# One stored order of q for scores and relative term, and stage one's norms and bound remainder at other places in the queues

## The reference

```python
q = split_heads(x @ Wq + bq)
k = split_heads(x @ Wk + bk)
v = split_heads(x @ Wv + bv)
scores = jnp.einsum('bhid,bhjd->bhij', q, k)
rel = jnp.einsum('bhid,pd->bhip', q, rel_key)
i = jnp.arange(s)[:, None]
j = jnp.arange(s)[None, :]
rel_idx = jnp.clip(j - i + p - 1, 0, p - 1)
bias = jnp.take_along_axis(rel, jnp.broadcast_to(rel_idx[None, None], (b, h, s, s)), axis=3)
causal = j <= i
logits = jnp.where(causal[None, None], (scores + bias) * scale, -jnp.inf)
attn = jax.nn.softmax(logits, axis=-1)
out = jnp.einsum('bhij,bhjd->bhid', attn, v)
```

## Time and profile before

| what | value |
|---|---|
| median of 3 runs | 739.33 us (736.46 to 739.54) |
| the profiled execution, its own time | 737.71 us |
| its span, first to last instruction | 735.6 us |
| stage one (to the first exponential of stage two) | 107.45 us |
| stage two (to the first matmul of stage three) | 107.45 to 526.89 us |
| mean granted TensorE clock | 0.947 of full speed |

### The profile page before, as it was taken

The page is one execution under the profiler, slowest core; times in us unless marked ns, Lnnn a source line. Parts: engine busy times, 40 slices in busy tenths (PEclk is TensorE's granted clock), DMA queues, the critical chain, the costliest instruction groups (busy, mean ns, idle before and its releaser), DMA issues.

```text
span 735.6 us, 18944 instructions
## 1 busy us (share of the span) xinstructions
PE 645.0 (88%) x8066; PEld 467.9 (64%) x8066; DVE 538.9 (73%) x923; ACT 572.5 (78%) x660; POOL 246.6 (34%) x175
## 2 busy tenths in 40 slices
PE   4877669999999999999999999978799898998993
PEld 2333336676766766867667667655588687786682
DVE  5885787787687877786877777765677568588546
ACT  2794977988989889889898898786577868677573
POOL 2100270360640912705408128010271441731801
PEclk9988767999999999999999999997999999999997
DMA  7487423152241231521412314040300000000001
GB/s 229 113 228 219 134 84 90 38 129 66 51 111 40 71 96 35 130 69 43 106 52 68 100 34 123 27 158 1 101 1 1 0 1 1 1 29 0 6 24 59
DMA packets 39175, 52.82 MB, mean 72 GB/s; under 512 B 5656, under 2 KB 29640, under 8 KB 36680
## 3 DMA queue, kind: packets, MB, share of 16 engines
q1 hardware_dynamic: 39088, 51.58, 25.6%
HBM read 39.00 MB, written 11.81 MB: 69 GB/s over the span
## 4 chain that ended last, share of the span: by engine, by line
PE 53%; DVE 13%; ACT 12%; issue 5%; POOL 2%; DVEq 0%; ACTq 0%; POOLq 0%
PE p_o L1114 16%; PE p_s L1089 13%; PE p_z L1788 8%; PE p_z L1791 8%; DVE probs L1215 6%; ACT probs L1332 6%; PE p_s L1023 5%; POOL hid_lo L1709 1%; DVE res L1969 1%; ACT hid_hi L1892 1%; ACT o_acc L1341 1%; ACT even_b L1036 1%; ACT odd_b L1036 1%; PE p_o L1126 1%; DVE hid_lo L1993 1%
## 5 line engine op out<-in xcount | busy, mean ns | idle before, releaser
L1089 PE MATMUL p_s<-q_sb,k_sb 96*128 96x128 bf16 (+1 forms) x1600 | 172.2, 250 | 9.2 <-ACT probs L1332 3.5
L1332 ACT ACTIVATE probs<-p_s 128x1024 f32<-128x1024 f32 x160 | 156.6, 1017 | 18.5 <-DVE p_s L1224 10.8
L1114 PE MATMUL p_o<-probs,v_sb 128*32 128x128 f32 (+1 forms) x3200 | 159.7, 331 | 7.5 <-ACT o_acc L1341 4.7
L992 POOL TENSOR_SCALAR_AFFINE_SELECT even_b<-even_b 128x2048 f32<-128x2048 f32 x31 | 75.9, 2449 | 259.6 <-ACT even_b L1036 259.6
L1332 ACT ACTIVATE probs<-probs 128x1024 f32<-128x1024 f32 x128 | 133.5, 1055 | 36.1 <-DVE probs L1215 35.8
L1089 PEld LDWEIGHTS p_s<-q_sb,k_sb 96*128 96x128 bf16 x1600 | 113.9, 100 | 68.5 <-issue 30.3
L1215 DVE TENSOR_TENSOR probs<-p_s,even_b 128x1024 f32<-128x1024 f32 x96 | 114.9, 1218 | 16.8 <-PE p_s L1089 16.8
L1114 PEld LDWEIGHTS p_o<-probs,v_sb 128*32 128x32 f32 x3200 | 84.6, 111 | 40.9 <-issue 13.9
L1788 PE MATMUL p_z<-hid_hi,h_hi 128*128 128x512 f32 x256 | 102.1, 399 | 1.7 <-POOL hid_lo L1709 1.7
L1023 PE MATMUL p_s<-q_rows,rel_w 72*128 72x64 bf16 x2048 | 83.8, 196 | 19.6 <-DVE probs L1215 8.7
L1791 PE MATMUL p_z<-hid_lo,h_hi 128*128 128x512 f32 x256 | 100.9, 394 | 0.0
(11 more groups left out here) (182 smaller groups left out, 846.2 us busy)
## 6 DMA issues: line engine op xcount, KB each, us to landing
k_sb<-k_dram SPq DMA_DIRECT2D x48, 192.0 KB
q_sb<-q_dram SPq DMA_DIRECT2D x16, 576.0 KB
q_rows<-qr_dram SPq DMA_DIRECT2D x42, 192.0 KB
q_dram<-q_parts SPq DMA_DIRECT2D x12, 256.0 KB, 3.0
k_dram<-k_parts SPq DMA_DIRECT2D x12, 256.0 KB, 3.2
qr_dram<-q_turned SPq DMA_DIRECT2D x12, 256.0 KB, 3.4
x_all<-in_L_attn_x_dram SPq DMA_DIRECT2D x4, 512.0 KB, 4.4
every<-in_L_ffn_h_w_dram SPq DMA_DIRECT2D x2, 1024.0 KB, 8.3
```

The source lines that it names most:

```text
L992: nc.gpsimd.affine_select(out=far, in_=near, compare_op=ALU.is_ge, fill=0.0, base=-1 - r, pattern=[[0, QB], [-1, MCH * RCH]], channel_mult ...
L1089: last = nc.tensor.matmul(slot[:, c:c + n * BLK], k_sb[hg][:, h * S + j * BLK:h * S + (j + 1) * BLK], ap(q_sb[hg], at, [[HG * S, KROWS], [ ...
L1114: last = nc.tensor.matmul(p_o[32 * h:32 * h + 32, at:at + blocks * BLK], v_sb[hg][:, j, h * 32:(h + 1) * 32], probs[n % PBUFS][:, h, col * ...
L1332: nc.scalar.activation(to, got, ACT.Exp, scale=SCALE).then_inc(t_exp, 1)
```

## The change

One layout of q serves both uses. Place i*128 + r*4 + l of a head (block i, group r of four places, l within the group) now lies at r*32 + i*4 + l: groups of four places of one block, eight blocks side by side. The q parts and the bound's parts are written in this order, `q_rows` is loaded from `q_dram`, and `q_turned`, `qr_dram` and their twelve copies and twelve stores are gone. The two matmuls that read q get other steps on their moving side. The sign of the bound's parts changes (the padding row is -1 now). In stage one `layernorm` of batch b+2 stands at the end of batch b, ahead of `gap` and `shift_rest` of batch b; `low_bits` comes after the middle parts, and `root` between the two halves of ACT's part of the bound. The branch for large scores gets a copy of q back into the natural order.

```diff
+LO = 4
...
-            sp.dma_start(to, ap(qr_dram, u * (UH * S) + half * width,
+            sp.dma_start(to, ap(q_dram, u * (UH * S) + half * width,
...
-    def turned_view(to, part):
-
-        return to[:, part, :].rearrange("p (r i) -> p r i", i=NB)
-
-    def untouched_view(got, part):
-
-        return got[:, part, :].rearrange("p (i r) -> p r i", i=NB)
+    def natural(tile):
+
+        return tile.rearrange("p (i r l) -> p r i l", i=NB, l=LO)
+
+    def mixed(tile):
+
+        return tile.rearrange("p (r i l) -> p r i l", i=NB, l=LO)
+
+    def mixed_half(tile, j):
+
+        return tile.rearrange("p (r i l) -> p i r l", i=NB, l=LO)[:, j * (NB // 2):(j + 1) * (NB // 2)]
 
...
-                for done in (s_qst, s_kst, s_rst):
+                for done in (s_qst, s_kst):
                     sp.wait_ge(done, 16 * PARTS)
-                sp.dma_start(q_rows[:, :], ap(qr_dram, 0, [[DROW, PARTS * HD], [0, PARTS], [1, UH * S]])).then_inc(t_qr[0], 16)
+                sp.dma_start(q_rows[:, :], ap(q_dram, 0, [[DROW, PARTS * HD], [0, PARTS], [1, UH * S]])).then_inc(t_qr[0], 16)
...
-                if not last:
-                    turned(b, part)
...
-        for part in range(PARTS):
-            turned(B - 1, part)
...
-            nc.vector.scalar_tensor_tensor(out=m_parts[:, 1, :], in0=p_tr[0:H, :], scalar=-1.0, in1=m_parts[:, 0, :],
-                                           op0=ALU.mult, op1=ALU.subtract).then_inc(s_mr, 1)
+            nc.vector.tensor_tensor(mixed(m_parts[:, 1, :]), natural(p_tr[0:H, :]), mixed(m_parts[:, 0, :]),
+                                    ALU.subtract).then_inc(s_mr, 1)
...
-            if not last_batch:
-                layernorm(b + 1, False, None if first else lambda: gap(b - 1))
-            else:
+            if not first:
                 gap(b - 1)
-            if not first:
                 shift_rest(b - 1)
...
-            nc.vector.tensor_tensor(q_rest[:, :], qf[:, :], q_parts[:, 0, :], ALU.subtract).then_inc(s_rest, 1)
+            nc.vector.tensor_tensor(mixed(q_rest[:, :]), natural(qf[:, :]), mixed(q_parts[:, 0, :]), ALU.subtract).then_inc(s_rest, 1)
...
+            if b + 2 < B:
+                layernorm(b + 2, False)
...
+        layernorm(1, False)
...
-        def turn_query(b, part):
-            act.wait_ge((s_hi, s_mid, s_low)[part], b * 2 + 1)
-            if b > 0 and part == 0:
-                act.wait_ge(s_rst, 16 * PARTS * b)
-            nc.scalar.activation(turned_view(q_turned, part), untouched_view(q_parts, part),
-                                 ACT.Identity).then_inc(s_turned, 1)
-
         def batch(b, first, last_batch):
...
-            if not first and not last_batch:
-                root(b + 1)
...
-            if b < CHECKS:
-                low_bits(b)
...
-            nc.scalar.activation(q_parts[:, 0, :], qf[:, :], ACT.Identity).then_inc(s_hi, 1)
+            nc.scalar.activation(mixed(q_parts[:, 0, :]), natural(qf[:, :]), ACT.Identity).then_inc(s_hi, 1)
             act.wait_ge(s_kf, b + 1)
             nc.scalar.activation(k_parts[:, 0, :], kf[:, :], ACT.Identity).then_inc(s_hi, 1)
-            if not last_batch:
-                turn_query(b, 0)
...
-            if not last_batch:
-                turn_query(b, 1)
-
+
+            if b < CHECKS:
+                low_bits(b)
             if not first:
                 act.wait_ge(s_mst, b * 16)
             for j in range(2):
+                if j == 1 and b + 2 < B:
+                    root(b + 2)
                 act.wait_ge(s_u, b * 2 + j + 1)
-                nc.scalar.activation(m_parts[:, 0, j * 512:(j + 1) * 512], p_tr[0:H, j * 512:(j + 1) * 512],
-                                     ACT.Identity, scale=-1.0).then_inc(s_mneg, 1)
-            if not last_batch:
-                turn_query(b, 2)
+                nc.scalar.activation(mixed_half(m_parts[:, 0, :], j),
+                                     p_tr[0:H, j * 512:(j + 1) * 512].rearrange("p (i r l) -> p i r l", i=NB // 2, l=LO),
+                                     ACT.Identity).then_inc(s_mneg, 1)
             if last_batch:
                 for c in range(FIRST_BEFORE, FIRST_ACT):
                     copy_act(act, "even", c)
                 nc.scalar.activation(exp_warm[:, :], ident[:, 0:1], ACT.Exp, scale=0.0)
-                turn_query(b, 0)
-                turn_query(b, 1)
-                turn_query(b, 2)
 
         root(0)
         transposed(0, True)
...
-        q = q_rows[:, :].rearrange("k (h r i) -> k r h i", h=UH, i=NB)
+        q = q_rows[:, :].rearrange("k (h r i l) -> k r l h i", h=UH, i=NB, l=LO)
...
-            last = nc.tensor.matmul(slot[:, x * QB:(x + 1) * QB], rel_w[0:ROWS, w0:w0 + BLK], q[:, r, :, :],
+            last = nc.tensor.matmul(slot[:, x * QB:(x + 1) * QB], rel_w[0:ROWS, w0:w0 + BLK], q[:, r // LO, r % LO],
                                     start=True, stop=True)
         last.then_inc(t_rel, 1)
 
@@ -1085,10 +1058,10 @@
...
-                    at = h * S + i * BLK
+                    at = h * S + i * LO
...
-                                            ap(q_sb[hg], at, [[HG * S, KROWS], [2 * BLK, n], [1, BLK]]),
+                                            ap(q_sb[hg], at, [[HG * S, KROWS], [2 * LO, n], [NB * LO, BLK // LO], [1, LO]]),
...
-            if u == 0 and hg == 0:
-                act.wait_ge(s_rst, 16 * PARTS * B)
...
```

40 lines of the change are left out of this document (18 added, 22 removed).

## The result

The changed kernel is slower: median 779.16 us (778.72 to 781.02, 4 runs) against 738.08 us (736.46 to 739.54, 4 runs) for the kernel before on the same chip, a ratio of 1.056 (95% interval 1.0537 to 1.0581). The forecast of 730 had the sign wrong, and the time lies far outside its range. The profiled execution took 779.4 us, with a span of 777.5.

A forecast was written before the change was run, and what follows sets the result against it. TensorE was taken to set the pace in stage two, a chain of handovers in stage one. The profiled 737.7 us less 9.5 (6.8 + 2.7) is 728.2; plus 1.6 for the median, 729.8, said as 730; range 725 to 739.5, the forecast's own 727 to 733.

The forecast's parts named there:

- TensorE's moving reads: Stage two's 1920 relative matmuls and the scores: reads in new steps cost nothing; bounds nothing to 110 us in all.
- The slow rival: Stage two: TensorE pays for steps of 8 bytes, 29 ns a matmul, 56 us, kernel 786 us; chance 0.12.
- the 9.5 us of stage one: Stage one's whole gain: 6.8 from an earlier start of batch 3's bound plus 2.7 from its shorter matmuls.
- GpSimd's masks: End of stage one: six masks start at 79.8, end at 98.1, 2.0 us before DVE's first biased addition is due.
- The bound of batch 3: End of stage one, on PE: starts near 82.2, takes 5.4 us instead of 8.1 at the upper clock, 2.7 gained.
- its first rival: Stage one: clock stays low in batch 3, or stores land later; 732.5 to 735 us, chance 0.13.
- The stores: Batch 1, stage one: eight stores become six, the awaited one lands near 68.0 instead of 72.0, 4.0 us gained.
- `kf` of batch 3: Stage one, on ACT: ends at 77.1, 7.4 us earlier, 3.4 of it from the three copies.
- the handover of batches 0 and 1: Stage one, DVE: `root` no longer behind a turned copy; 1.0 us less in batch 0, 1.7 in batch 1.
- Writes in the new order: Stage one, `q_parts` part 0 and `q_rest`: 16-byte f32 read runs cost nothing; up to 3.6 us at 0.9 each.
- the last three copies: End of stage one, ACT: 5.80 us of turned copies under the longer DVE chain, so removing them is worth nothing there.

The follow-up runs named there:

- e3: The changed kernel with groups of two places instead of four (LO = 2): 840.59 us, a single run.
- e4: The changed kernel with groups of eight places instead of four (LO = 8): 930.56 us, a single run.
- e6: The kernel before, turned copies kept, with only the change's new places for layernorm, root and low_bits: 738.74 us, 1.0004 of before.
- e5: The kernel of e1, with GpSimd's masks of the opening chunks waiting until DVE has made the last `own`: 732.22 us, 0.991 of before.
- e2: The kernel before, with only the scores reading runs of four places 64 bytes apart (of other places): 737.43 us, a single run.
- e1: The changed kernel, but the relative matmuls read 64 neighbouring columns (values of other places): 737.1 us, 0.999 of before.

## Why the prediction was wrong, step by step

**TensorE's moving reads: the step that failed.** The prediction took nothing, on the strength of `values`: 4 bytes a value at 0.26 ns each, "1.04 ns for each 16 bytes", a ceiling of 6 ns. That inference doesn't carry. It counts four streams that run side by side as one. Taken one by one, each of them has 64 pieces of 16 bytes in four times 67 ns, that is 4.2 ns a piece (my estimate from the same row), so the row never spoke against a price below that. e3 and e4 measured it: 1.74 ns, whatever the clock. The row of ACT that was set aside as farther off had it nearly right: it gave 29 ns a matmul and 56 us, against 28 and 54. The slow rival had mechanism, place and price of a matmul, and a chance of 0.12. That its 786 is so near the 779 measured is partly luck: it still counts the 9.5 us of stage one, which did not come, and all 56 of stage two, of which 41 came, since 8 went into idling that was there anyway. The prediction itself called this step the deciding one and its bounds were 0 and 110 us; to pick the lower one from a row of another operation was the error.

**GpSimd's masks: a step left out.** The prediction asked of the masks only whether they end in time (2.0 us of cover). It moved them from 87.85 to 79.8 (81.04 measured) without asking what runs beside them there, though its own numbers had DVE's selection between 77.6 and 82.1, beside the first of them. In the traces of before and of e6 they miss the selections by 0.16 us. In e5 the correction is worth 4.9 us of 737.1 by the medians and 2.6 in stage one of the two profiled executions, a quarter to a half of what the forecast gave stage one.

**The bound of batch 3: mis-sized.** Forecast 5.4 us at the upper clock, bought by short idling. In e5 it took 7.25 with 3.0 us of idling before it. Both ends of this term were in the prediction, and the one against it was also its first rival. What was off is the idling: 0.9 us was forecast, before the relative chunks (1.05 in e5), but the 3.0 between them and the bound were not in the sum, and after these the matmuls ran at the lower level.

**The stores: the mechanism right, the gain about half.** ACT goes on at 69.77, still waiting for the store: 2.25 us earlier than before where 4.0 were forecast. The window from 44 to 72 moved 187 GB/s and not the 216 that the forecast used, a miss that it had allowed for (2.5 us for a tenth of the rate). e6 shows the same from the other side: with eight stores the earlier batches gain nothing.

**`kf` of batch 3: the number right, 77.25 for 77.1, by luck.** Two misses cancel. The store came 1.8 later, and PE's bound of batch 2 ended at 71.35 rather than 74.5, so that ACT did not wait for it, as the forecast had it, but ran through. The transposes of batch 3 started at 58.19 and not 60.8, and 1.7 of these 2.6 are the earlier start of the execution (`rstd` at 19.69 instead of 21.38). Counted from there, the remainder of batch 0 came 1.2 us earlier than before (19.29 us after it instead of 20.53; forecast 1.0), and from remainder to remainder DVE needed 17.85 us (forecast 18.5). So the handover of batches 0 and 1 was right, and a little better than forecast.

**Writes in the new order, and the last three copies: right.** `q_parts` takes 1.06 and `q_rest` 1.22 where no mask runs beside it, and the scores' runs of 8 bytes are free (e2).

**The sum.** The profiled execution of before, 737.7, with stage two 41.2 longer and stage one 0.65 longer gives 779.6; the profiled one of after took 779.4. With the read undone (e1), stage one's 9.5 is 1.8 in the profile (first exponential 105.61), and with the masks held (e5) 4.4. The first may be off by the 1.3 us that e1 started earlier (`rstd` at 20.08), the second by 0.1 (21.26).

## What to carry to other kernels

When a layout is shared by two readers, count for each how many of its values lie in every 16 bytes, and bound the price by a row of an engine that really reads with such steps; a dense read of the same engine proves nothing about it. Where the reader is the engine that sets the pace, 28 ns on each of 1920 instructions (54 us) outweigh the 24 us of copies that are saved on an engine with room. And when work is moved forward, look at what GpSimd does at the new time: an operation of 0.25 us there took 2.4.

## What the runs showed of the hardware that I had not expected

- TensorE's moving read needs about 1.74 ns for each further 16 bytes, at either clock. With four bf16 values in each, a chunk is all but free (0.65 us against 0.63), with two it takes 1.08, with one 1.97.
- ACT reads two bf16 values per 16 bytes nearly at full pace (1.12 us for 1024 columns against 1.05). Reading them 256 bytes apart takes 1.99, and *writing* one every 16 bytes 4.78. Written runs of four values cost nothing (1.06).
- In these traces a mask of GpSimd held up even an addition of 128x2 numbers until it ended (0.16 us became 1.74), and the next masks took the next operations: 4.72 us for two selections of 0.2.
- The granted clock fell to its lower level in a stretch where PE counts as 98% busy (groups of eight, mean 0.81), when the relative term with its slow moving read had 40% of that busy time (229.5 of 569.7 us). That the slow read is the cause wasn't tried by itself.
